# Outputs of a retention layer: the cross product joined with half of the inner one, both query decays moved to 64 partitions, and one turned operand given its own memory

## The chip, the cores and the metric

The kernel runs on 1 core of one Trainium2 chip. The metric is the device time of one execution in microseconds (us). Engines are named as the profile names them: PE (TensorE, matmul), PEld (its weight loads), DVE (VectorE), ACT (ScalarE), POOL (GpSimd), SP (SyncE, which issues most DMAs).

## The reference, cut to what matters

x is 4 sequences of 1024 tokens by 1024 channels. A layer norm gives xn. From xn come a ternary-weight product with a SiLU (the gate g) and a retention layer s; the result is x + s * g. The retention layer works over 16 heads of 64 dimensions in chunks of 128 tokens, with a state S of 64 x 64 per head that passes from chunk to chunk:

```python
mask  = where(t >= s, exp(-s_h * (t - s)), 0)          # per head, 128 x 128, lower triangle
lam_t = exp(-s_h * t); lam_rev = exp(-s_h * (T - t)); lam_T = exp(-s_h * T)
scores = einsum('bhtd,bhsd,hts->bhts', qi, ki, mask)
intra  = einsum('bhts,bhsd->bhtd', scores, vi)
cross  = einsum('bhtd,ht,bhde->bhte', qi, lam_t, S)
o      = scale * (intra + cross)
S      = lam_T * S + einsum('bhtd,ht,bhte->bhde', ki, lam_rev, vi)
```

The output o is normalised (RMS, twice, folded into one scale per token), projected by ternary weights and multiplied by the gate.

## The kernel before, in words

The 4096 tokens are worked in 16 blocks `i` of 256 tokens, each of 2 chunks `c` of 128 tokens; `g = 2 i + c` numbers the chunks. A sequence is 8 chunks (4 blocks). Chunks 0, 8, 16 and 24 are first in their sequence and have no state to take over; so 28 of the 32 chunks have a cross product. Blocks 0 to 2 are worked in one order, from block 3 on in another ("by tokens"), and in blocks 4 to 14 the projection is done by 7 products instead of 8 ("by products").

Each engine has its program written out by hand, in order, with semaphores between them. In one block from 4 on, PE does: the q projections of the block (L854), the k and v products (L839, L813) mixed with the projection of the block before (L1012), then for c = 0: `scores` (L892, q times k, transposed: source tokens are partitions, query tokens are columns), a v and an ffn product (L813, L787), `turn_k` (L904), `outputs` (L938 and L942), `update_state` (L919), ffn products; then for c = 1: `scores`, an ffn product, `output_scale` (L964: sums of squares of the first chunk's outputs, through `total_of`), ffn products with `spread_gamma` (L973) among them, `outputs`, and the projection of the first chunk. In a block whose first chunk is first in its sequence (4, 8, 12) `output_scale` stands half a product later, and in blocks 3 and 15 a whole product later.

`outputs` makes, for each pair of heads r and each head e of the pair, 64 rows of `att_ps` (64 dimensions by 128 tokens) from two f32 products. The cross product (L938) has `state` as weights, 128 partitions by 64 columns, with zeros in the half of the other head, and `q_decay` as moving operand. The inner product (L942) has `v_tok` (128 tokens by 64 columns) as weights and `scores_m` as moving operand; both move 128 columns. An f32 product stands as two records in the trace.

DVE masks the scores (`mask_scores`, L1523, four instructions a chunk, one for each half of the heads and each e), weights the outputs (`weight_o`, L1581), adds the new part to the state (`add_state`, L1567), splits operands into high and low halves (L1362, L1597), combines rows (L1378, L1608), and finishes k and v (`add_k` L1407, `add_v` L1399). PE's last k product, "p4", waits for the second `add_k` of the block; the last v product "p4" for the second `add_v`; `output_scale` on PE waits for the sums that POOL makes (`sum_squares`, L2506 to L2515).

POOL runs in this order in such a block: `add_out` (L2532), `output_scale` of the block before (L2521, L2525), `norm_scale` of the next block (L2385 to L2404), `decay_q(i, 0)` in two halves (L2481), more `add_out`, `decay_state(i, 0)` (L2493), `bias_z` (L2466, L2468), `decay_q(i, 1)` in two halves, `sum_squares(i, 0)`, `output_scale(i, 0)`, `decay_state(i, 1)`, `sum_squares(i, 1)`. In block 1 POOL also subtracts ffn and v weights (L2416, L2428), which keeps it busy from 144 us on; `decay_q(1, 0)`, `decay_state(1, 0)` and `decay_q(1, 1)` stand in that row ahead of `output_scale(1, 0)`.

`b_turned`, an operand of the k and v products, is written by ACT (`weigh_b`, L2009) and lies in the same memory as `scores_m`.

Of the kernel before, what the change touches and what calls it, by code (L numbers as in the profile page):

```python
# [36 lines left out]
def program(nc, x, qkv_w, proj_w, decay, ffn_w, ffn_b, norm_cols, x_turned, out):  # L37
# [17 lines left out]
    with ExitStack() as ctx:  # L55
# [34 lines left out]
        QL_OFF = V_OFF + CHUNKS * C  # L90
        ST_OFF = QL_OFF + 2 * C
        SM_OFF = ST_OFF + 2 * PR * P
        ARENA = SM_OFF + H * T
# [4 lines left out]
        with nc.sbuf_tensor("arena", [P, ARENA], F32) as arena:  # L98
            pass
        sb("arena_low", [P, SM_OFF])  # L100

        o_row = sb("o_row", [P, CPH, T])
        o_split = sb("o_parts", [P, 3, 2, CPH, T], F16)
# [26 lines left out]
        v_tok = arena[:, V_OFF:QL_OFF].rearrange("p (c n) -> p c n", c=CHUNKS)  # L130
        q_decay = arena[:, QL_OFF:QL_OFF + C].rearrange("p (r t) -> p r t", r=PR)
        k_decay = arena[:, QL_OFF + C:QL_OFF + 2 * C]

        ow_first = k_decay.rearrange("p (r t) -> p r t", r=PR)
        state = arena[:, ST_OFF:SM_OFF].rearrange("p (k r e) -> p k r e", k=2, r=PR)
        scores_m = arena[:, SM_OFF:ARENA].rearrange("p (h e r t) -> p h e r t", h=HALF, e=2, r=CPH)

        b_turned = arena[:, SM_OFF:ARENA].rearrange("p (c j t) -> p c j t", c=CHUNKS, j=NCB)
# [7 lines left out]
        lam_T = sb("lam_T", [P, PR])  # L146
# [13 lines left out]
        diag = sb("diag", [P, CHUNKS, T])  # L160

# [36 lines left out]
        s_state0 = sem("state_zeroed")  # L198
# [138 lines left out]

        def passes_on(g):

            return g - g // NCHUNK  # L340
# [5 lines left out]
        def of_half(i, c, h):  # L346
            return chunk(i, c) * HALF + h + 1

# [347 lines left out]
        def tensor_program(pe):  # L696
# [514 lines left out]
        def vector_program(dve):  # L1211
# [297 lines left out]
            def mask_scores(i, c):  # L1509
# [5 lines left out]
                if c == 0 and i > 0 and by_products(i - 1):  # L1515

                    dve.wait_ge(s_ops, of_o_product(i - 1, "p3"))
                for half in range(HALF):
                    dve.wait_ge(s_sc, HALF * g + half + 1)
# [30 lines left out]
            def add_state(i, c):  # L1550
# [3 lines left out]
                if n == 0:  # L1554
                    dve.wait_ge(s_state0, 1)
# [3 lines left out]
                else:  # L1559
                    dve.wait_ge(s_sd, 2 * (passes_on(g) - (g // NCHUNK + 1)) + 2)  # L1560
# [1234 lines left out]
```

## Time and profile before

| | |
|---|---|
| runs of the kernel | 1314.46 us median of 3 (1314.1 to 1314.81) |
| profiled execution, first to last instruction | 1314.2 us |
| granted TensorE clock over the span | 1.000 |
| PE busy | 1289.1 us (98%) |
| PEld busy | 824.8 us (63%) |
| DVE busy | 1008.4 us (77%) |
| ACT busy | 617.4 us (47%) |
| POOL busy | 600.4 us (46%) |
| share of PE in the chain that ended last | 94% |

Busy time of PE counts every moment in which a matmul is in the array; matmuls overlap, so the duration of one in the rows (its time through the array) is longer than its distance from the next. The chain of work gives the distances. In the timeline, a row is a run of like instructions on one engine: its start, its length, the count, and in brackets the idle time before it with what ended it.

### The profile page before, as it was taken

The page shows a single profiled execution, that of the slowest core. Times are in us where ns is not written, and L with a number is a line of the kernel's source. Part 1 is how long each engine was busy: PE and PEld are TensorE (multiplying, and loading weights), DVE is VectorE, ACT ScalarE, POOL GpSimd, SP SyncE. Part 2 cuts the span into 40 slices and gives each one's busy share as a digit, 9 for nine tenths or more (in the row PEclk, how much of TensorE's full clock was granted, in tenths as well). Part 3 has the DMA queues.
Part 4 walks back from the last instruction along what each step waited for, and adds up shares of the span by engine and source line. Part 5 has one row for each costly group of instructions (what it writes and reads, how often), then busy time and mean ns, then how long its engine had stood idle before and what let it go on. Part 6 is the DMA issues. An engine that isn't in the chain of part 4 may idle for free.

```text
span 1314.2 us, 25908 instructions
## 1 busy us (share of the span) xinstructions
PE 1289.1 (98%) x10263; PEld 824.8 (63%) x10263; DVE 1008.4 (77%) x1567; ACT 617.4 (47%) x1216; POOL 600.4 (46%) x537
## 2 busy tenths in 40 slices
PE   4999999999999999999999999999999999999998
PEld 2577767675665757566574656657566575756655
DVE  7888367687676887878788787877878788787755
ACT  5884144344434635446354544644436363544621
POOL 1442785955354435354432535435333443535352
PEclk9999999999999999999999999999999999999999
DMA  9631101203012030210303011030300304021020
GB/s 361 248 97 66 57 34 37 101 33 106 1 38 100 17 121 18 76 46 18 121 17 120 18 57 65 17 121 18 94 28 19 119 17 121 17 58 49 1 65 32
DMA packets 33433, 90.32 MB, mean 69 GB/s; under 512 B 10529, under 2 KB 10785, under 8 KB 33314
## 3 DMA queue, kind: packets, MB, share of 16 engines
q1 hardware_dynamic: 33024, 88.65, 20.0%
q8 instruction: 82, 1.34, 0.4%
q14 instruction: 37, 0.30, 0.1%
q10 hardware_dynamic: 290, 0.02, 0.0%
HBM read 71.85 MB, written 16.81 MB: 67 GB/s over the span
## 4 chain that ended last, share of the span: by engine, by line
PE 94%; DVE 2%; ACT 2%; DMA 1%; issue 1%; SPq 0%; POOL 0%; DVEq 0%; ACTq 0%; POOLq 0%
PE ring L854 20%; PE ring L787 13%; PE ring L813 13%; PE ring L839 12%; PE ring L1012 10%; PE ring L988 5%; PE att_ps L892 4%; PE att_ps L942 4%; PE att_ps L938 4%; PE ring L904 2%; PE att_ps L919 2%; PE ring L867 1%; PE ring L754 1%; DMA raw<-in_ffn_w 1%; ACT junk L1951 1%
## 5 line engine op out<-in xcount | busy, mean ns | idle before, releaser
L854 PE MATMUL ring<-b_lo,qkv_q 128*128 128x256 f16 x1216 | 268.2, 272 | 0.0
L854 PE MATMUL ring<-b_hi,qkv_q 128*128 128x256 f16 x1216 | 268.2, 273 | 0.0
L2532 POOL TENSOR_TENSOR xt<-xt,gate_even 128x512 f32<-128x512 f32 x58 | 90.6, 1564 | 172.5 <-DVE gate_even L1626 131.8
L854 PEld LDWEIGHTS ring<-b_hi,qkv_q 128*128 128x128 fp8e4 x1216 | 120.2, 99 | 15.8 <-issue 0.4
L854 PEld LDWEIGHTS ring<-b_lo,qkv_q 128*128 128x128 fp8e4 x1216 | 118.9, 98 | 15.6
L2506 POOL TENSOR_TENSOR sq<-sq,cols 128x1024 f32<-128x1024 f32 x29 | 55.0, 1896 | 126.8 <-DVE b_lo L1423 118.6
L2094 ACT ACTIVATE gate_even<-gate_even 128x512 f32<-128x512 f32 x60 | 37.3, 625 | 136.2 <-DVE gate_even L1454 136.1
L942 PE MATMUL att_ps<-arena 128*64 128x128 f32 x1024 | 95.0, 273 | 0.0
L938 PE MATMUL att_ps<-arena 128*64 128x128 f32 x896 | 88.5, 276 | 0.0
L1523 DVE TENSOR_TENSOR arena<-att_ps,mask 128x512 f32<-128x512 f32 x128 | 79.3, 680 | 11.0 <-PE att_ps L892 11.0
L2385 POOL TENSOR_TENSOR ln<-ln,small 128x3 f32<-128x3 f32 x32 | 37.4, 1168 | 100.2 <-DVE ln L1311 99.3
L2481 POOL TENSOR_TENSOR arena<-arena,lam_q 128x512 f32<-128x512 f32 x56 | 77.2, 1398 | 9.7 <-ACT arena L2110 7.0
L1454 DVE SCALAR_TENSOR_TENSOR gate_even<-ring,ln,gate_even 128x512 f32<-128x512 f32 x70 | 52.4, 748 | 29.0 <-PE ring L787 29.0
L2466 POOL TENSOR_TENSOR gate_even<-gate_even,bias 128x512 f32<-128x512 f32 x14 | 19.8, 1415 | 114.0 <-ACT gate_even L2070 113.9
L2110 ACT ACTIVATE arena<-ring,wscale 128x512 f32<-128x512 f32 x64 | 43.4, 679 | 58.0 <-PE ring L854 58.0
L892 PEld LDWEIGHTS att_ps<-arena 64*128 64x128 f32 x1024 | 59.7, 188 | 13.8 <-issue 13.8
L2493 POOL TENSOR_TENSOR arena<-arena,lam_T 64x512 f32<-64x512 f32 x48 | 61.6, 1283 | 13.5 <-DVE arena L1565 10.8
L892 PE MATMUL att_ps<-arena 64*128 64x128 f32 x1024 | 65.8, 278 | 0.5 <-ACT sq L2136 0.5
L1648 DVE SCALAR_TENSOR_TENSOR gate_even<-ring,wscale,gate_even 128x512 f32<-128x512 f32 x36 | 27.0, 749 | 50.7 <-PE ring L1012 36.2
L942 PEld LDWEIGHTS att_ps<-arena 128*64 128x64 f32 x1024 | 63.5, 137 | 0.7 <-issue 0.7
L2521 POOL TENSOR_TENSOR small<-small 128x1 f32<-128x1 f32 x32 | 18.5, 580 | 99.5 <-DVE small L1633 99.5
L787 PE MATMUL ring<-ffn_q,a_lo 128*128 128x512 fp8e4 x168 | 63.6, 379 | 0.0
(298 smaller groups left out, 3523.1 us busy)
## 6 DMA issues: line engine op xcount, KB each, us to landing
xt<-in_x SPq DMA_DIRECT2D x60, 512.0 KB, 3.7
out<-xt SPq DMA_DIRECT2D x31, 512.0 KB, 2.7
raw<-in_qkv_w SPq DMA_DIRECT2D x24, 512.0 KB, 15.8
y<-in_x_turned SPq DMA_DIRECT2D x14, 512.0 KB, 5.9
y_odd<-in_x_turned SPq DMA_DIRECT2D x14, 512.0 KB, 6.7
raw<-in_ffn_w SPq DMA_DIRECT2D x8, 512.0 KB, 9.8
norm_rows<-norm_out SPq DMA_DIRECT2D x14, 256.0 KB, 6.0
raw<-in_proj_w SPq DMA_DIRECT2D x6, 512.0 KB, 4.7
```

Of the source, the lines that this page charges most:

```text
L787: ins = pe.matmul(ring[:, b, :], of[:, j, :], weights_of(weights)[:, j, :], start=(begins and j == 0 and k == 0), stop=(j == CPH - 1 and k ...
L813: ins = pe.matmul(ring[:, b, :], of[:, j, :], v_weights_of(weights)[:, j, :], start=(name in ("p1", "p5") and j == 0 and k == 0), stop=(j ...
L839: ins = pe.matmul(ring[:, b, :], of[:, j, :], k_weights_of(weights)[:, j, :], start=(name in ("p1", "p5") and j == 0 and k == 0), stop=(j ...
L854: ins = pe.matmul(ring[:, b, e * BT:(e + 1) * BT], qkv_q[:, cb, o:o + P], part[:, cb, :], start=(cb == 0 and part is b_hi and (e == 0 or i ...
L892: ins = pe.matmul(att_ps[:, 2 * half + e, j, :], k_t[rows, r, ts], q_t[rows, r, ts], start=True, stop=True)
L938: pe.matmul(att_ps[e * D:(e + 1) * D, half, j, :], state[:, passes_on(g) % 2, r, e * D:(e + 1) * D], q_decay[:, r, :], start=True, stop=Fa ...
L942: ins = pe.matmul(att_ps[e * D:(e + 1) * D, half, j, :], v_tok[:, c, r * P + e * D:r * P + (e + 1) * D], scores_m[:, half, e, j, :], start ...
L988: ins = pe.matmul(ring[:, b, :], part[:, cb, :], proj_q[:, cb, cs], start=(cb == 0 and k == 0), stop=(cb == NCB - 1 and k == 1))
L1012: ins = pe.matmul(ring[:, b, :], of[:, j, :], proj_weights_of(weights)[:, j, :], start=(name in ("p1", "p5") and j == 0 and k == 0), stop= ...
L1523: dve.tensor_tensor(scores_m[:, half, e, :, :], att_ps[:, 2 * half + e, :, :], mask[:, e, half * CPH:(half + 1) * CPH, :], ALU.mult).then_ ...
L2481: pool.tensor_tensor(q_decay[:, hs, :], q_t[:, hs, c * T:(c + 1) * T], lam_q[:, hs, :], ALU.mult).then_inc(s_ql, 1)
L2532: pool.tensor_tensor(o, o, gate_of(i)[:, c, cs], ALU.add).then_inc(s_add, 1)
```

## The change

For a chunk that is not first in its sequence, a new buffer `v_state` holds, per head, 64 tokens of v on partitions 0 to 63 and the head's state on partitions 64 to 127. A new buffer `stack` holds per head three pieces of 64 columns: piece 0 has the masked scores of the early 64 query tokens (partitions 0 to 63; the early queries see no later sources) over the decayed q of the early tokens (partitions 64 to 127); piece 1 the masked scores of the late 64 query tokens on all 128 partitions; piece 2 zeros over the decayed q of the late tokens. One product of `v_state` over pieces 0 and 2 (128 columns) gives the cross product of all tokens and the inner product of the early ones; one product of v over piece 1 (64 columns) adds the inner product of the late ones.

The state now lies on partitions 64 to 127 for both heads of a pair, without the zeros. `decay_q` becomes two POOL instructions on 64 partitions by 1024 elements, one per head of the pair, both after the whole outputs of the chunk before; `decay_state` becomes one instruction of 64 partitions by 1024 instead of two of 64 by 512. The first 64 tokens of v are copied into `v_state` by a DMA of 256 KB that ACT issues, one for each such chunk. `b_turned` gets its own memory, and `weigh_b` no longer waits for the outputs of the block before.

```diff
             def outputs(i, c, half):
...
-                if not is_first(g):
-                    pe.wait_ge(s_ql, HALF * takes_over(g) + half + 1)
-                    if half == 0:
-                        pe.wait_ge(s_st, 2 * passes_on(g))
+                if not is_first(g) and half == 0:
+                    pe.wait_ge(s_ql, 2 * takes_over(g) + 2)
+                    pe.wait_ge(s_st, 2 * passes_on(g))
+                    pe.wait_ge(s_vcopy[c], copied(i, c))
...
-                    if not is_first(g):
+                    to = [att_ps[e * D:(e + 1) * D, half, j, :].rearrange("p (s t) -> p s t", s=2) for e in range(2)]
+                    v = [v_tok[:, c, r * P + e * D:r * P + (e + 1) * D] for e in range(2)]
+                    if is_first(g):
                         for e in range(2):
-                            pe.matmul(att_ps[e * D:(e + 1) * D, half, j, :],
-                                      state[:, passes_on(g) % 2, r, e * D:(e + 1) * D], q_decay[:, r, :],
-                                      start=True, stop=False, skip_group_check=True)
+                            ins = pe.matmul(to[e], v[e], stack[:, e, r, 0:2, :], start=True, stop=True)
+                        continue
+
                     for e in range(2):
-                        ins = pe.matmul(att_ps[e * D:(e + 1) * D, half, j, :],
-                                        v_tok[:, c, r * P + e * D:r * P + (e + 1) * D],
-                                        scores_m[:, half, e, j, :], start=is_first(g), stop=True,
-                                        skip_group_check=True)
+                        pe.matmul(to[e], joined(g)[:, r, e, :], stack[:, e, r, 0:3:2, :],
+                                  start=True, stop=False, skip_group_check=True)
+                    for e in range(2):
+                        ins = pe.matmul(to[e][:, 1, :], v[e], stack[:, e, r, 1, :],
+                                        start=False, stop=True, skip_group_check=True)
...
             def mask_scores(i, c):
...
+                early = slice(0, P if is_first(g) else D)
...
-                    for e in range(2):
-                        dve.tensor_tensor(scores_m[:, half, e, :, :], att_ps[:, 2 * half + e, :, :],
-                                          mask[:, e, half * CPH:(half + 1) * CPH, :], ALU.mult).then_inc(s_scm, 1)
+                    for s, rows in enumerate((early, slice(0, P))):
+                        ts = slice(s * D, (s + 1) * D)
+                        dve.tensor_tensor(stack[rows, :, hs, s, :], att_ps[rows, 2 * half:2 * half + 2, :, ts],
+                                          mask[rows, :, hs, ts], ALU.mult).then_inc(s_scm, 1)
...
             def add_state(i, c):
...
                 for e in range(2):
-                    rows, cs = slice(e * D, (e + 1) * D), slice(e * D, (e + 1) * D)
-                    to = state[rows, (n + 1) % 2, :, cs]
+                    rows = slice(e * D, (e + 1) * D)
+                    to = v_state[D:P, (n + 1) % 2, :, e, :]
...
             def weigh_b(i, c):
 
-                act.wait_ge(s_o, HALF * (chunk(i - 1, 1) + 1))
+                if c == 0 and i > 2:
+                    act.wait_ge(s_bslo, of_b_sum(i - 1, "S4"))
+                    if by_products(i - 2):
+                        act.wait_ge(s_ops, of_o_product(i - 2, "p3"))
...
+            def copy_v(i, c):
+
+                g = chunk(i, c)
+                if is_first(g):
+                    return
+                for by in v_at(i, c):
+                    act.wait_ge(*by)
+                if g > 1:
+                    act.wait_ge(s_o, HALF * (g - 1))
+                else:
+                    act.wait_ge(s_wout, w_n["qkv", QKV_TILES - 1])
+                act.dma_start(joined(g)[0:D, :, :, :].rearrange("p r e d -> p (r e d)"),
+                              v_tok[0:D, c, :]).then_inc(s_vcopy[c], DMA)
...
             def attention_by_tokens(i, c):
                 if c == 0:
                     take_v(i, 1)
+                    copy_v(i, 1)
                     base_z(i)
...
-            def decay_q(i, c, half):
+            def decay_q(i, c):
                 g = chunk(i, c)
                 if is_first(g):
                     return
-                n = takes_over(g)
-                hs = slice(half * CPH, (half + 1) * CPH)
-                pool.wait_ge(s_q, CPH * i + 2 * (half + 1))
...
-                if n > 0:
-                    pool.wait_ge(s_o, HALF * (g - 1) + half + 1)
-                pool.tensor_tensor(q_decay[:, hs, :], q_t[:, hs, c * T:(c + 1) * T], lam_q[:, hs, :],
-                                   ALU.mult).then_inc(s_ql, 1)
+                pool.wait_ge(s_q, CPH * (i + 1))
...
+                pool.wait_ge(s_o, HALF * g)
...
+                for e in range(2):
+                    rows = slice(e * D, (e + 1) * D)
+                    q, by = (of.rearrange("p r (s t) -> p r s t", s=2)
+                             for of in (q_t[rows, :, c * T:(c + 1) * T], lam_q[rows, :, :]))
+                    pool.tensor_tensor(stack[D:P, e, :, 0:3:2, :], q, by, ALU.mult).then_inc(s_ql, 1)
+                    pool.wait_ge(s_ql, 2 * takes_over(g) + e + 1)
...
             def decay_state(i, c):
...
-                for e in range(2):
-                    rows, cs = slice(e * D, (e + 1) * D), slice(e * D, (e + 1) * D)
-                    pool.tensor_tensor(state[rows, (n + 1) % 2, :, cs], state[rows, n % 2, :, cs],
-                                       lam_T[rows, :].unsqueeze(2).to_broadcast([D, PR, D]), ALU.mult).then_inc(s_sd, 1)
-
-                    pool.wait_ge(s_sd, 2 * (n - g // NCHUNK - 1) + e + 1)
+                to, of = (v_state[D:P, k % 2, :, :, :].rearrange("p r e d -> p (r e) d") for k in (n + 1, n))
+                pool.tensor_tensor(to, of, lam_T[D:P, :].unsqueeze(2).to_broadcast([D, H, D]),
+                                   ALU.mult).then_inc(s_sd, 1)
+                pool.wait_ge(s_sd, decays(g))
```

In blocks from 3 on, `copy_v(i, 0)` stands on ACT's queue behind the high parts of the next block's b and ahead of `take_v(i, 1)`. No call on POOL's queue moves: `decay_q(i, c, 0)` and `decay_q(i, c, 1)` become `decay_q(i, c)` where they stood.

## Rows read from the trace of the kernel before

**Rows 1.** The page: the chain that ended last, shares by engine.
```profile
PE 94%; DVE 2%; ACT 2%; DMA 1%; issue 1%; SPq 0%; POOL 0%; DVEq 0%; ACTq 0%; POOLq 0%
```

**Rows 2.** The chain of work in block 6: start us, us, what.
```profile
573.06 0.22 PE att_ps L942 x4
573.28 0.93 PE att_ps L919 x32
574.21 3.56 PE ring L787 x16
```

**Rows 3.** POOL's instructions by line and shape: busy us, mean ns of one.
```profile
L2493 POOL TENSOR_TENSOR arena<-arena,lam_T 64x512 f32<-64x512 f32 x48 | 61.6, 1283 | 13.5 <-DVE arena L1565 10.8
L2506 POOL TENSOR_TENSOR sq<-sq,cols 128x1024 f32<-128x1024 f32 x29 | 55.0, 1896 | 126.8 <-DVE b_lo L1423 118.6 <-ACT sq L2136 8.2
L2510 POOL TENSOR_TENSOR sq<-sq 128x512 f32<-128x512 f32 x29 | 36.8, 1271 | 2.3
L2510 POOL TENSOR_TENSOR sq<-sq 128x256 f32<-128x256 f32 x29 | 21.1, 729 | 2.3
```

**Rows 4.** Timeline of POOL, block 6, chunk 0 to chunk 1.
```profile
573.20 2.51 POOL L2481 TENSOR_TENSOR arena<-arena,lam_q 128x512 f32<-128x512 f32 x2
575.66 1.90 POOL L2506 TENSOR_TENSOR sq<-sq,cols 128x1024 f32<-128x1024 f32 x1
579.86 0.46 POOL L2515 TENSOR_TENSOR sq_sum<-sq 128x128 f32<-128x128 f32 x1
583.66 2.16 POOL L2493 TENSOR_TENSOR arena<-arena,lam_T 64x512 f32<-64x512 f32 x2
```

**Rows 5.** Timeline: PE's output_scale in blocks 6 and 4, POOL's last sum in 4.
```profile
581.45 0.38 PE L964 MATMUL att_ps<-small,sq_sum 128*128 128x1 f32 x2
423.71 0.45 POOL L2515 TENSOR_TENSOR sq_sum<-sq 128x128 f32<-128x128 f32 x1
424.43 0.28 PE L964 MATMUL att_ps<-small,sq_sum 128*128 128x1 f32 x2
```

**Rows 6.** Timeline of POOL, DVE and PE, start of block 6.
```profile
537.94 2.94 POOL L2481 TENSOR_TENSOR arena<-arena,lam_q 128x512 f32<-128x512 f32 x2
537.97 1.78 DVE L1378 TENSOR_TENSOR y_odd<-y,y_odd 128x512 f32<-128x512 f32 x1
539.67 1.75 DVE L1362 TENSOR_TENSOR a_lo<-y,a_hi 128x512 f16<-128x512 f32 x1
542.17 0.68 DVE L1362 TENSOR_TENSOR a_lo<-y,a_hi 128x512 f16<-128x512 f32 x1
546.63 0.74 DVE L1407 SCALAR_TENSOR_TENSOR gate_odd<-ring,wscale,gate_odd 128x512 f32<-128x512 f32 x1
547.97 0.38 PE L839 MATMUL ring<-k_sum_last,b_hi 128*128 128x512 fp8e4 x1
551.63 0.75 DVE L1648 SCALAR_TENSOR_TENSOR gate_even<-ring,wscale,gate_even 128x512 f32<-128x512 f32 x1 [2.87 <-PE ring L1012]
```

**Rows 7.** Timeline of POOL and PE in block 1.
```profile
189.05 0.38 POOL L2525 TENSOR_SCALAR diag<-ident,small 128x128 f32<-128x128 f32 x1
190.03 0.49 PE L973 MATMUL ring<-diag,mean_sq 128*128 128x128 f32 x2
```

**Rows 8.** Timeline of block 7: DVE's split of o, then PE's next product.
```profile
666.73 1.22 DVE L1597 TENSOR_TENSOR o_lo<-arena,o_hi 128x1024 f16<-128x1024 f32 x1
668.21 0.39 PE L1012 MATMUL ring<-proj_q,o_hi 128*128 128x512 fp8e4 x1
```

**Rows 9.** DMA issues of the page: count, KB each, median us to landing.
```profile
out<-xt SPq DMA_DIRECT2D x31, 512.0 KB, 2.7
y_odd<-in_x_turned SPq DMA_DIRECT2D x14, 512.0 KB, 6.7
```

**Rows 10.** Timeline of DVE and PE around outputs of block 6, chunk 0.
```profile
563.68 1.40 DVE L1399 SCALAR_TENSOR_TENSOR arena<-ring,wscale,arena 128x512 f32<-128x512 f32 x2
569.57 0.44 PE L938 MATMUL att_ps<-arena 128*64 128x128 f32 x4
```

More of the change, by code:

```diff
@@ L97, in program @@
             pass
[L98 to L103, printed above, removed]
+        arena = sb("arena", [P, ARENA])
         SQ = 2 * PR * T
@@ L160, in program @@
         diag = sb("diag", [P, CHUNKS, T])
+        with nc.sbuf_tensor("b_turned", [P, CHUNKS, NCB, T], F32) as b_turned:
+            pass
+        o_row = sb("o_row", [P, CPH, T])
+        o_split = sb("o_parts", [P, 3, 2, CPH, T], F16)
         wsum = diag[:, 0, 0:5 * NCB]
@@ L197, in program @@
         s_ident, s_iota, s_cut = sem("ident_made"), sem("iotas_made"), sem("mask_cut")
-        s_state0 = sem("state_zeroed")
+        s_zeros = sem("stack_zeros_set")
+        s_vcopy = [sem(f"v_copied{c}") for c in range(CHUNKS)]
         s_ones, s_peak = sem("constants_set"), sem("peak_taken")
@@ L336, in is_last, with decays @@
             return g % NCHUNK == NCHUNK - 1
+        def decays(g):
+            return sum(not is_first(k) and not is_last(k) for k in range(g + 1))
         def passes_on(g):
@@ L347, in of_half, with copied, joined @@
             return chunk(i, c) * HALF + h + 1
+        def copied(i, c):
+            return DMA * sum(not is_first(chunk(k, c)) for k in range(i + 1))
+        def joined(g):
+            return v_state[:, passes_on(g) % 2, :, :, :]
         def of_ffn(i, c, h):
@@ L1514, in mask_scores @@
                     dve.wait_ge(s_wout, w_n["qkv", QKV_TILES - 1])
-                if c == 0 and i > 0 and by_products(i - 1):
-                    dve.wait_ge(s_ops, of_o_product(i - 1, "p3"))
+                early = slice(0, P if is_first(g) else D)
                 for half in range(HALF):
+                    hs = slice(half * CPH, (half + 1) * CPH)
                     dve.wait_ge(s_sc, HALF * g + half + 1)
@@ L2108, in qk_out @@
                     elif j == 0:
-                        act.wait_ge(s_ql, HALF * takes_over(chunk(i, 0)))
+                        act.wait_ge(s_ql, 2 * takes_over(chunk(i, 0)))
                     act.activation(q_t[:, r:r + 2, :], bank, ACT.Copy, scale=wscale[:, 7:8]).then_inc(s_q, 1)
@@ L2473, in decay_q @@
                     return
[L2474 to L2477 removed]
+                pool.wait_ge(s_q, CPH * (i + 1))
+                if takes_over(g) == 0:
                     pool.wait_ge(s_tables, TABLES)
[L2479 to L2482 removed]
+                pool.wait_ge(s_o, HALF * g)
+                if c == 1:
+                    pool.wait_ge(*((s_zeros, 1) if i == 0 else (s_vwsum, 3) if i == 1 else (s_zbias, HALF * (i - 1))))
+                elif i + 1 == NB:
+                    pool.wait_ge(s_gamma, chunk(i - 1, 1) + 1)
+                elif by_products(i - 1):
+                    pool.wait_ge(s_beta, chunk(i + 1, 1) + 1)
+                else:
+                    pool.wait_ge(*((s_pwsum, 1) if i == BY_PRODUCTS - 1 else (s_add, of_out(i - 1, 1, 1))))
+                for e in range(2):
[4 more added lines that the diff above has]
+                    pool.wait_ge(s_ql, 2 * takes_over(g) + e + 1)
             def decay_state(i, c):
@@ L2559, in attention @@
                             sum_v_weights(name)
-                    decay_q(i, 1, 0)
-                    decay_q(i, 1, 1)
+                    decay_q(i, 1)
                 else:
@@ L2605, in gpsimd_program @@
             pool.wait_ge(s_wout, w_n["qkv", QKV_TILES - 1])
-            pool.memset(state, 0.0).then_inc(s_state0, 1)
+            pool.memset(stack[0:D, :, :, 2, :], 0.0).then_inc(s_zeros, 1)
             for i in range(NB):
@@ L2624, in gpsimd_program @@
                     if by_products(i - 1):
-                        decay_q(i, 0, 0)
-                        decay_q(i, 0, 1)
+                        decay_q(i, 0)
                         add_out(i - 1, 1, 1)
@@ L2639, in gpsimd_program @@
                             sum_proj_weights("T4")
-                        decay_q(i, 0, 0)
-                        decay_q(i, 0, 1)
+                        decay_q(i, 0)
                 attention(i, 0)
```

42 lines of the change are left out of this document (27 added, 15 removed).

## The prediction

> **What bounds the kernel now.** I read the page's chain of work first: 94% of it is PE [rows 1], and PE is busy for 98% of the span. So a microsecond taken from PE's own work is a microsecond of time, as long as nothing that PE waits for comes later than it does now. Next I read the chain in order of time inside one block (block 6, a middle one), to see what one product costs in distance and not in its pipelined length: two heads with 128 moving columns take 0.22 us, and the 16 products of update_state, weights of the same shape (128 by 64) with 64 moving columns, take 0.93 us together, 0.116 us a pair [rows 2]. Then I read POOL's timeline between the two chunks of a block against PE's [rows 4, 5], because the change puts work on POOL, and last the start of a block, where POOL and DVE meet [rows 6]. The averages (POOL 46% busy, DVE 77%) say nothing here: what matters is how long before PE each result is there. For POOL's sums that is 581.45 less 580.32, 1.1 us, in a middle block, and 424.43 less 424.16, under 0.3 us, in a block that opens a sequence [rows 4, 5].
>
> **What the change takes from PE.** Per pair of heads, two products of 128 columns for two heads (0.22 + 0.22) become one of 128 and one of 64 (0.22 + 0.116): 0.104 saved, 0.83 us for the 8 pairs of a chunk. 28 chunks have a cross product: 23.2 us. The first chunks of the four sequences keep one product of 128 columns and save nothing. Bounds: exactly half of 0.22 would give 24.6 us; if weight loads set the pace the saving is smaller (rival D).
>
> **What it adds to POOL.** decay_q was two instructions of 128 x 512, 2.46 us for both (573.20 to 575.66) [rows 4]. Now it is two of 64 x 1024. What sets a POOL instruction's time is the elements per partition and how many full operands it reads: 256 take 0.729 us and 512 take 1.271, so 2.12 ns an element [rows 3], and 1024 take 1.271 + 512 x 0.00212 = 2.36 us. The number of partitions does not help: with one broadcast operand, 64 x 512 twice takes 2.16 [rows 4], 1.08 each, and 128 x 1024 takes 1.90 [rows 3], again by elements per partition. Two of 2.36, with about 0.1 for the waits that the new code puts behind each, make 4.85 us: 2.4 us more for each call. No row has this shape; the lower bound is 1.90 an instruction (the broadcast form), the upper 2.54 (twice 1.271). decay_state becomes one instruction like the 1.90 row instead of 2.16: 0.26 less.
>
> **Where that lands, between the chunks.** decay_q(i, 1) begins when POOL is free, with no idle time ahead of it [rows 4], so its waiting for the whole of outputs(i, 0) costs nothing (those end 0.8 us earlier than now). What is queued behind it is sum_squares(i, 0), and PE's output_scale waits for that. The sums come 2.4 us later; PE arrives 0.83 us earlier; the slack was 1.1. PE waits 2.4 + 0.8 - 1.1 = 2.1 us in blocks 5, 6, 7, 9, 10, 11, 13 and 14: 17 us. In blocks 4, 8 and 12 outputs(i, 0) save nothing and the slack is under 0.3: 2.2 each, 6.5 us. In blocks 3 and 15 output_scale stands a whole ffn product later (3.56 / 2 = 1.8 us [rows 2]): 0.3 each, 0.6 us. Blocks 0 and 2 have room.
>
> **Block 1** has both calls on a POOL that is never idle. PE's spread_gamma there has 190.03 - 189.43 = 0.6 us of slack [rows 7]; POOL comes to it 2 x 2.4 - 0.26 = 4.5 later. So it falls 3.9 us behind, and the 1.7 that the block's outputs save is swallowed too: 5.6 us of waiting.
>
> **At the start of a block.** decay_q(i, 0) runs beside DVE work in which both inputs lie in SBUF, and DVE is held while a POOL instruction runs: two DVE instructions take 1.78 and 1.75 us where the same form takes 0.68 unhindered [rows 6]. Each POOL instruction holds one of them; with POOL's each 1.1 longer, DVE falls 2.2 us behind. The DVE work up to the second add_k (L1407) is without idle time, and PE's last k product waits for that: it ends at 547.37 and PE starts at 547.97 [rows 6]. So PE waits about 2.2 - 0.55 = 1.65 us, in the blocks 5, 6, 7, 9, 10, 11, 13, 14 that have this order: 13.2 us. After it DVE has 2.87 us of idle time [rows 6], so the lateness goes no further. Bounds: nothing if the collision falls elsewhere, 16 us if the upper POOL price holds. Blocks 2, 3 and 15 have the collision in another place; I take 1 us for them together.
>
> **After outputs(i, 1).** PE's next product in blocks 7 and 11 needs DVE's split of o, which is there 668.21 - 667.95 = 0.26 us ahead [rows 8]; with outputs 0.83 shorter PE waits 0.6 in each, and about 0.4 in blocks 2, 3 and 15: 2.3 us.
>
> **At nothing.** The mask stays four DVE instructions of 512 elements. The adding of the state keeps its shape and writes other partitions. The DMA of v: ACT issues it when add_v of the chunk is done, 564.4 us, and outputs begin at 569.57 [rows 10], 5.1 us later; 512 KB out of SBUF land in 2.7 us, the slowest kind in the rows in 6.7 [rows 9], and this is 256 KB. I take it as hidden; uncovered it would cost up to 1.6 us in some 9 chunks. ACT waits at that point for DVE ahead of take_v(i, 1), whose product isn't ready before. The waits taken from weigh_b and from the first mask of a block are already passed in the order of those queues (ACT squares the outputs of the block before ahead of weigh_b), so b_turned's own memory gives nothing.
>
> For such a copy the Trainium skill (DMA: Bandwidth & Descriptors, Anatomy of one DMA) gives a fixed 2.0 us plus bytes over 436 GB/s, an estimate of 2.6 us here; by it the copy is hidden as well, and no row of this trace has an SBUF-to-SBUF copy.
>
> **Sum.** -23.2 + 17 + 6.5 + 0.6 + 5.6 + 13.2 + 1 + 2.3 = +23.0 us against the profiled span of 1314.2; the median of the runs is 0.3 above it. Forecast 1337 us, 1.7% slower: PE's saving is real and is more than spent in waits for POOL and for DVE held up by POOL.
>
> **Rivals.** *A, POOL late but DVE not held longer.* The 13.2 and the 1 fall away: 1323 us. For it: the collision depends on which engine gets in first. Against: all eight blocks show the same two long DVE rows.
>
> *B, POOL not late (the other side).* If a POOL instruction's time goes by all its elements, 64 x 1024 costs what 128 x 512 did, 1.27, and every wait above but the last goes: 1314.2 - 23.2 + 2.3 = 1293 us, 1.6% faster. It decides at the length of the pair of decays: under 2.7 us (2.46 + what is left of the slack, 1.1 - 0.83) PE does not wait in a middle block; the whole change breaks even with the pair at about 3.75 (some 21 pairs on the path share the 23 us). Against it speaks that 64 x 512 is no cheaper per column than 128 x 1024 [rows 3, 4]. At the lower bound of 1.90 each the pair is 0.9 shorter: 11 x 0.9 + 1.8 + 8 x 0.9 off the sum, about +4 us, 1318.
>
> *C, the copy of v is late.* With 6.7 us to landing outputs(i, 0) start 1.6 later in 9 chunks; most of it comes off the wait at output_scale behind it, so some +4 us: 1341.
>
> *D, weight loads pace the 64-column product,* so that columns save little. Then the saving before output_scale was lost anyway, and 16 x 0.83 = 13 us in second chunks is not had: about 1348. Against it speaks update_state, same weights and 64 columns, at half the distance [rows 2].
>
> The Trainium skill's rule for a stream of weight load and matmul (TensorE: Matmul & The Clock Gate, Back-to-back issue gap) speaks for D: it gives about 81 ns a matmul at 128 columns and 131 at 512, so 64 columns fewer save some 8 ns of a record. By that estimate 448 products of two records each would save 7 us in place of 23. The trace does not follow it: a record here takes 55 ns at 128 columns and 29 at 64 [rows 2].
>
> **Chances.** The forecast with both waits (1327 to 1345): 0.52. A, or the lower POOL bound with a little of each (1317 to 1327): 0.22. Within 0.2% of before, 1312 to 1317: 0.05. B and partial gains, below 1312: 0.12. C, D and worse, above 1345: 0.09. The range 1311 to 1345 holds 0.8; the likeliest alone has 1327 to 1345. Differences under 0.2% (2.6 us) can't be told from none for this kernel. Faster 0.12, same 0.05, slower 0.83.
>
> **What would show it.** In the profile after: the joined product and the 64-column one at 0.22 and 0.11 to 0.12 a pair in the chain; the decay_q group at 2.3 to 2.5 us mean, 56 of them; idle time on PE ahead of output_scale, released by POOL's sum, about 2 us in 11 blocks; idle time ahead of the last k product, released by add_k, about 1.7 us in 8; DVE's L1378 and L1362 rows near 2.9 us where they were 1.78 and 1.75. The prediction is wrong if POOL's pair takes under 3.75 us, if PE shows no idle time at output_scale, or if the 64-column products stand 0.2 apart.

## The result, and the profile after

The changed kernel takes 1357.18 us (median of 4 runs, 1355.65 to 1358.16); the kernel before, timed beside it, 1314.63 (4 runs). The ratio is 1.032, with a 95% interval from 1.031 to 1.034. The change makes the kernel 3.2% slower. The forecast had the direction, at 1337 us, but the time is 12 us above the top of its range. The profiled execution's span is 1356.9 us, 42.7 more than before.

The page of the changed kernel: busy time of PE, the chain that ended last, two groups of instructions (busy us, mean ns of one, idle time before them) and the DMA of v.

```profile
PE 1289.5 (95%) x10263; PEld 809.5 (60%) x10263; DVE 1032.9 (76%) x1567; ACT 616.4 (45%) x1216; POOL 661.8 (49%) x513
...
PE 58%; DVE 17%; POOL 16%; issue 4%; ACT 2%; DMA 2%; SPq 0%; DVEq 0%; POOLq 0%; ACTq 0%
...
L2531 POOL TENSOR_TENSOR arena<-arena,lam_q 64x1024 f32<-64x1024 f32 x56 | 139.5, 2491 | 26.1 <-PE att_ps L953 11.8
...
L798 PE MATMUL ring<-ffn_q,a_hi 128*128 128x512 fp8e4 x168 | 69.3, 413 | 0.0
...
arena<-arena ACTq DMA_DIRECT2D x28, 256.0 KB, 3.0
```

PE's share of the chain fell from 94% [rows 1] to 58%: the chain now goes through POOL's q decays and DVE's work. PE's waits, in the view of waits (us in total, times, longest):

```profile
PE att_ps L980 <- POOL sq_sum L2569: 25.3, 13, 2.3
PE ring L746 <- DVE y L1339: 12.4, 2, 11.6
PE ring L850 <- DVE gate_odd L1423: 9.3, 8, 1.2
PE ring L989 <- POOL diag L2579: 2.6, 2, 2.1
...
PE att_ps L957 <- POOL arena L2531: 2.1, 1, 2.1
PE ring L824 <- DVE arena L1415: 1.8, 1, 1.8
PE ring L746 <- DVE small L1649: 1.5, 1, 1.5
PE ring L1028 <- DVE o_lo L1613: 1.1, 2, 0.5
```

All waits of that view sum to 64.3 us, and to 22.1 in the same view of the kernel before: 42.2 more. The 12.4 at the start were there before:

```profile
PE ring L735 <- DVE y L1323: 12.5, 2, 11.7
```

But TensorE also saves time, so waits alone don't close the account. What is missing stands in the chain in order of time, between the chunks of block 6 (start us, us, what), where [rows 4, 5] were taken before:

```profile
587.44 2.34 POOL arena L2531
...
589.86 2.36 POOL arena L2531
...
592.28 1.91 POOL sq L2560
...
596.47 0.46 POOL sq_sum L2569
...
597.07 0.35 PE att_ps L980 x2
597.42 4.30 PE ring L798 x12
601.71 0.22 PE att_ps L989 x2
```

PE waits for the last sum until 597.07. Then twelve products take 4.30 us where the same chain of the kernel before has 2.61, which is 0.22 a product, the pace of the sixteen in [rows 2]:

```profile
581.83 2.61 PE ring L787 x12
```

The windows of that stretch (us, then busy time of PE, PEld, DVE, ACT and POOL, each with the number of instructions that touch the window, then granted clock, DMA share and GB/s):

```profile
597.00:598.00 1.00, 0.94 (x5) 0.57 (x6) 0.16 (x1) 0.00 (x0) 0.31 (x1) 0.76 0.00 0
598.00:599.00 1.00, 1.00 (x4) 0.32 (x3) 0.00 (x0) 0.00 (x0) 0.72 (x3) 0.50 0.00 0
599.00:600.00 1.00, 1.00 (x3) 0.29 (x2) 0.00 (x0) 0.00 (x0) 1.00 (x1) 0.50 0.00 0
600.00:601.00 1.00, 1.00 (x4) 0.43 (x3) 0.32 (x1) 0.00 (x0) 0.82 (x1) 0.53 0.00 0
601.00:602.00 1.00, 1.00 (x8) 0.61 (x7) 0.43 (x1) 0.54 (x1) 0.00 (x0) 1.00 0.00 0
```

And one of the same products in the kernel before:

```profile
583.00:584.00 1.00, 1.00 (x6) 0.47 (x5) 0.38 (x1) 0.00 (x0) 0.82 (x3) 1.00 0.00 0
```

PE is busy in every one of these microseconds from 597 on, but from 598 to 601 only 3 or 4 products touch each in place of 6: they start 0.43 apart in the timeline where the kernel before has 0.22. The granted clock is 0.50 there, the lower of TensorE's two levels (1.2 of 2.4 GHz). Going through the whole trace in windows of 1 us, this happens 11 times, and the clock missing (1 less the granted clock, summed) is 1.7 us each time, 18.8 together; before, 0.3, at the very end. Eight of them stand behind waits at output_scale (blocks 5 to 10, 13, 14), and three in blocks 0 and 1. This makes the busy time of PE misleading: it is 1289.5 us although 23 us of columns went away, because products at the lower clock are longer (L798 has a mean of 413 ns; 379 in the last kernel below, whose clock never falls).

The account of the 42.7 us, then: 42.2 of waits, 18.8 of clock, some 3.5 for starting again (the product after a wait takes 0.17 longer in the chain, as in 1.90 for 8 products of L850 where 1.73 is usual, and there are about 21 new waits; an estimate), less 22.7 for the products (28 chunks by 0.81, below): 41.8.

### The profile page after: what moved, and what is told of

Read it like the earlier page. It is cut to its first block, busy times and chain, and to the rows that moved or that the text cites. A ratio compares the mean times of both kernels' runs of the same rounds, so it can differ in the third digit from the quotient of the medians.

```text
span 1356.9 us, 25934 instructions
## 1 busy us (share of the span) xinstructions
PE 1289.5 (95%) x10263; PEld 809.5 (60%) x10263; DVE 1032.9 (76%) x1567; ACT 616.4 (45%) x1216; POOL 661.8 (49%) x513
## 4 chain that ended last, share of the span: by engine, by line
PE 58%; DVE 17%; POOL 16%; issue 4%; ACT 2%; DMA 2%; SPq 0%; DVEq 0%; POOLq 0%; ACTq 0%
PE ring L865 15%; PE ring L824 11%; PE ring L798 8%; PE ring L1028 6%; POOL arena L2531 5%; PE ring L850 5%; PE ring L1004 4%; DVE a_lo L1378 3%; POOL sq L2564 2%; PE att_ps L903 2%; POOL sq L2560 2%; PE att_ps L957 2%; DVE y L1394 2%; POOL gate_even L2507 1%; POOL gate_even L2509 1%
## 5 line engine op out<-in xcount | busy, mean ns | idle before, releaser
L2531 POOL TENSOR_TENSOR arena<-arena,lam_q 64x1024 f32<-64x1024 f32 x56 | 139.5, 2491 | 26.1 <-PE att_ps L953 11.8
L1539 DVE TENSOR_TENSOR arena<-att_ps,mask 128x512 f32<-128x512 f32 (+1 forms) x128 | 79.1, 675 | 10.6 <-PE att_ps L903 10.6
L957 PE MATMUL att_ps<-arena 128*64 128x128 f32 x896 | 80.8, 283 | 2.1 <-POOL arena L2531 2.1
L798 PE MATMUL ring<-ffn_q,a_lo 128*128 128x512 fp8e4 x168 | 69.6, 414 | 0.0
L798 PE MATMUL ring<-ffn_q,a_hi 128*128 128x512 fp8e4 x168 | 69.3, 413 | 0.0
L903 PEld LDWEIGHTS att_ps<-arena 64*128 64x128 f32 x1024 | 59.7, 188 | 13.7 <-issue 13.7
L960 PE MATMUL att_ps<-arena 128*64 128x64 f32 x896 | 65.1, 224 | 0.0
L2564 POOL TENSOR_TENSOR sq<-sq 128x512 f32<-128x512 f32 (+1 forms) x58 | 57.8, 997 | 4.5
L2088 ACT ACTIVATE gate_odd<-ring,wscale 128x512 f32<-128x512 f32 x26 | 17.9, 688 | 90.9 <-PE ring L850 90.9
## 6 DMA issues: line engine op xcount, KB each, us to landing
raw<-in_qkv_w SPq DMA_DIRECT2D x24, 512.0 KB, 15.8
```

Source lines behind the costliest of these rows:

```text
L798: ins = pe.matmul(ring[:, b, :], of[:, j, :], weights_of(weights)[:, j, :], start=(begins and j == 0 and k == 0), stop=(j == CPH - 1 and k ...
L903: ins = pe.matmul(att_ps[:, 2 * half + e, j, :], k_t[rows, r, ts], q_t[rows, r, ts], start=True, stop=True)
L957: pe.matmul(to[e], joined(g)[:, r, e, :], stack[:, e, r, 0:3:2, :], start=True, stop=False, skip_group_check=True)
L1539: dve.tensor_tensor(stack[rows, :, hs, s, :], att_ps[rows, 2 * half:2 * half + 2, :, ts], mask[rows, :, hs, ts], ALU.mult).then_inc(s_scm, 1)
L2531: pool.tensor_tensor(stack[D:P, e, :, 0:3:2, :], q, by, ALU.mult).then_inc(s_ql, 1)
L2564: pool.tensor_tensor(sq[:, 0, 0:m, :], sq[:, 0, 0:m, :], sq[:, 0, m:2 * m, :], ALU.add).then_inc(s_sqw, 1)
```

## The experiments

Each is compared with the kernel before on the same chip, where that took 1314.0 to 1317.3 us, so the ratios are what can be set side by side. Spans are those of the profiled executions.

**1. Keep TensorE busy through the wait.** In `output_scale` of the changed kernel, blocks 4 to 14:

```
+                if by_products(i) and c == 0:
+                    pe.wait_ge(s_alo, of_part(i, "S3"))
+                    for k in range(20):
+                        pe.matmul(att_bank(3)[:, 2 * P:4 * P], part_of("S3")[0][:, 0, :],
+                                  weights_of("T3")[:, 0, 0:2 * P], start=True, stop=True)
                 pe.wait_ge(s_red, sums(chunk(i, c)))
```

> The changed kernel, and in blocks 4 to 14 twenty matmuls of 256 columns whose results nobody reads, issued on TensorE just ahead of its wait for GpSimd's sum of squares of chunk 0. GpSimd and VectorE get no work more. Theory A (the change costs 43 us because GpSimd's longer q decays make TensorE wait 2.1 us in eleven blocks, and TensorE's clock falls to its lower level, 0.50, behind each such wait, worth 1.7 us each): TensorE is busy through the wait, the clock stays at 1.00, and the time falls by 11 x 1.7 = 18 us to some 1339 us, with the sum of squares as late as before. Theory B (the clock has no part in it; the 20 us that the forecast lacks are waits elsewhere): the time stays at 1357, or rises if the twenty matmuls outlast the wait.

Measured: 1344.5 us, ratio 1.021 (1.0195 to 1.0225), 14.0 us less span than the changed kernel (14.7 by the two ratios). PE's timeline in block 6:

```profile
592.39 2.36 PE L982 MATMUL att_ps<-ffn_q,a_hi 128*128 128x256 fp8e4 x20
594.58 0.28 PE L985 MATMUL att_ps<-small,sq_sum 128*128 128x1 f32 x2
594.73 0.38 PE L798 MATMUL ring<-ffn_q,a_hi 128*128 128x512 fp8e4 x1
594.94 0.38 PE L798 MATMUL ring<-ffn_q,a_lo 128*128 128x512 fp8e4 x1
```

And the windows of that stretch, with the clock in the third column from the end:

```profile
592.00:594.00 2.00, 2.00 (x18) 1.50 (x17) 1.08 (x2) 0.00 (x0) 1.78 (x3) 1.00 0.00 0
594.00:596.00 2.00, 2.00 (x15) 1.25 (x14) 0.16 (x1) 0.00 (x0) 1.13 (x3) 1.00 0.00 0
```

The sum comes as late as before, PE does 2.4 us of useless work, and the kernel is faster for it: products stand 0.21 apart again. The eight falls at this place are gone. The one in block 0 is gone too, although PE waits there as before (1.5 and 0.5 us), and block 1 has one stretch of 10.2 us at 0.50 where the changed kernel had two short ones. The missing clock is 5.1 us in place of 18.8, 13.7 less, and the span lost 14.0; the expected 18 had counted a fall at all eleven places. So the clock is shown as a cost of its own, apart from the wait.

**2. Half the q decay.** In `decay_q` of the changed kernel, with the stack zeroed once at the start:

```
-                    pool.tensor_tensor(stack[D:P, e, :, 0:3:2, :], q, by, ALU.mult).then_inc(s_ql, 1)
+                    pool.tensor_tensor(stack[D:P, e, 0:CPH, 0:3:2, :], q[:, 0:CPH], by[:, 0:CPH],
+                                       ALU.mult).then_inc(s_ql, 1)
```

> The changed kernel with both q decays over the first four of the eight head pairs only, so each instruction of GpSimd has 64 x 512 elements instead of 64 x 1024; the q decay of the other four pairs is left out (that part of the stack stays zero). TensorE's products are the same. Theory A (all of the loss is GpSimd's time): the pair of decays falls from 4.9 to 2.5 us, the wait ahead of the output scale and the 0.50 clock behind it go, and the 28 x 0.83 us that TensorE saves are seen whole: 1293 us, 1.6% under the kernel before. Theory B (the joined products or the copy of v cost more than their rows show, or TensorE's saving is eaten by the next wait): the time stays above 1310 us.

Measured: 1301.5 us, ratio 0.988 (0.987 to 0.990), clock 1.000. The waits for the sum fall to 0.5 us in all:

```profile
PE att_ps L980 <- POOL sq_sum L2571: 0.5, 3, 0.2
```

This is the case that rival B describes, brought about by leaving the decay of four of the eight head pairs out; what the new products save is real once POOL's work is short. The 1293 expected was some 6 us too good beyond the 2.3 by which this chip is slower: PE's waits sum to 27.7 us, 5.6 more than before, in small ones for DVE's and POOL's parts, 1.2 and 1.4 us long at the most.

**3. The kernel before, made late.** On POOL:

```
+                for _ in range(times):
+                    pool.tensor_tensor(q_decay[:, 0:CPH, :], q_t[:, 0:CPH, T:2 * T], lam_q[:, 0:CPH, :],
+                                       ALU.mult).then_inc(s_again, 1)
...
+                    repeat_q(i, 3 if by_products(i) else 0)
                     decay_q(i, 1, 0)
                     decay_q(i, 1, 1)
```

> The kernel before, with the first half of chunk 1's q decay written three times more on GpSimd in blocks 4 to 14 (128 x 512 elements, 1.27 us each, 3.8 us in all), ahead of the real one. Nothing of the change is in it. Theory A (lateness of GpSimd alone makes both the wait and the fall of the clock): waits of about 2.7 us in eight blocks and 3.5 us in blocks 4, 8 and 12, together 32 us, and behind each the clock at 0.50 for over 3 us, 11 x 1.7 = 18 us more: about 1365 us. Theory B (the slow stretch behind the wait belongs to the new products or to the changed layout): the waits alone, about 1347 us, and a clock of 1.00.

Measured: 1364.5 us (1359.5 to 1368.5), ratio 1.036 (1.033 to 1.039). The row of the view of waits:

```profile
PE att_ps L965 <- POOL sq_sum L2528: 34.1, 11, 3.8
```

The waits were as expected (34.1 us). The falls were not: 4 of the 11 in the profiled execution, behind the three waits of 3.8 us and behind one of the eight of 2.7 to 2.9. They cost the same 1.7 us each. The profiled execution is the fastest of the four, with a granted clock of 0.995. The others took 5 to 9 us more, and their granted clocks are on record as 0.990, 0.990 and 0.988: 13.6, 13.6 and 16.4 us of missing clock where the profiled one has 6.8, so about 8, 8 and 10 falls by an estimate from the 1.7. So lateness of POOL alone makes both costs, without any of the new products, and the clock's part of it is not the same in each execution.

**4. The sum ahead of the decay.** On POOL in the changed kernel:

```
-                if c == 1:
+                if c == 1 and not by_products(i):
                     sum_squares(i, 0)
...
+                    if by_products(i):
+                        sum_squares(i, 0)
+                        pool.wait_ge(s_red, sums(g))
                     decay_q(i, 1)
```

> The changed kernel with GpSimd's sum of squares of chunk 0 issued ahead of chunk 1's q decay in blocks 4 to 14, all its work kept. Theory A: the 25 us of waits for the sum and the 18 us of lower clock behind them go; TensorE waits instead about 1 us in each of the eleven blocks for the q decays of chunk 1, which end later: 1357 - 43 + 11 = about 1325 us, and 1314 if this wait is hidden. Theory B (the sum was only the first of several late things, and the decays are wanted as early): a wait of over 2 us at the outputs of chunk 1, the clock falls there instead, and the time stays at 1350 us or more.

Measured: 1343.7 us, ratio 1.021 (1.019 to 1.023). Both theories missed the place. The sum is in time, but POOL's `output_scale`, which makes the diagonal that PE wants next, is now what is queued behind the decay (PE's timeline, block 6):

```profile
596.42 0.49 PE L989 MATMUL att_ps<-diag,mean_sq 128*128 128x128 f32 x2 [1.69 <-POOL diag L2579]
```

Eight waits of 1.69 us and three of 2.30 took the place of eleven of 2.1 to 2.3: 4 us less. The rest of the gain is the clock: no fall behind any wait of 1.69, two behind those of 2.30, and missing clock of 5.1 us instead of 18.8. The span is 15.8 us shorter, for a reordering that took only 4 us off the waits. That it was their length that kept the clock up is not shown by this run; run 5 tries shorter waits in another kernel.

**5. Fewer repeats.** As 3, with `repeat_q(i, 2 if by_products(i) else 0)`.

> The kernel before with two repeats of the first half of chunk 1's q decay on GpSimd in blocks 4 to 14 where e3_late had three, 2.54 us in all. The sum of squares is 1.27 us less late than in e3_late, whose waits were 2.7 to 2.9 us in eight blocks and 3.8 in three. Theory A (the clock falls behind some waits of over 2 us and behind none of 1.7 or less): waits of 1.4 to 1.6 us in eight blocks and 2.5 us in blocks 4, 8 and 12, some 20 us, and a fall behind at most the three long ones, 1.7 us each: 1337 to 1342 us on a chip where the kernel before takes 1317. Theory B (any stop of TensorE at this place brings the clock down): 11 falls, 19 us more, 1356 us.

Measured: 1339.1 us, ratio 1.019 (1.017 to 1.020). Waits of 1.37 to 1.56 us with no fall, three of 2.43 with two falls. PE's timeline in blocks 4 and 5:

```profile
427.87 0.56 PE L965 MATMUL att_ps<-small,sq_sum 128*128 128x1 f32 x2 [2.43 <-POOL sq_sum L2528]
509.00 0.35 PE L965 MATMUL att_ps<-small,sq_sum 128*128 128x1 f32 x2 [1.55 <-POOL sq_sum L2528]
```

The windows behind these two waits:

```profile
428.00:429.00 1.00, 1.00 (x4) 0.55 (x5) 0.16 (x1) 0.00 (x0) 0.29 (x1) 0.50 0.00 0
510.00:512.00 2.00, 2.00 (x12) 1.08 (x10) 0.75 (x1) 0.08 (x1) 1.74 (x4) 1.00 0.00 0
```

These are theory A's figures, and they speak against theory B: a stop at this place doesn't always bring the clock down.

**6. The start of the block alone.** The edit of run 2, in chunk 0 only:

```
+                    pool.tensor_tensor(stack[D:P, e, 0:(PR if c else CPH), 0:3:2, :], q[:, 0:(PR if c else CPH)],
+                                       by[:, 0:(PR if c else CPH)],
+                                       ALU.mult).then_inc(s_ql, 1)
```

> The changed kernel with the q decay of chunk 0 of each block over four of the eight head pairs only (the other four are left out and stay zero); that of chunk 1 is whole. Theory A (the 9.3 us of waiting at the last k product come from GpSimd holding VectorE through its longer decays at the start of a block): these eight waits of 1.17 us go, and so do some 3 us of the waits in block 1; the waits for the sum of squares and the low clock behind them stay: 1357 - 12 = about 1345 us. Theory B (the last k product waits for something else that the change moved): 1354 to 1357 us.

Measured: 1346.7 us, ratio 1.022 (1.021 to 1.024), 10.0 us less span. The row of L850 is gone from the view of waits. DVE's timeline in block 6 of the changed kernel:

```profile
551.62 2.84 DVE L1378 TENSOR_TENSOR a_lo<-y,a_hi 128x512 f16<-128x512 f32 x1
554.59 2.61 DVE L1394 TENSOR_TENSOR y<-y_odd,y 128x512 f32<-128x512 f32 x1
```

And the same two in this kernel:

```profile
548.88 1.76 DVE L1378 TENSOR_TENSOR a_lo<-y,a_hi 128x512 f16<-128x512 f32 x1
550.78 1.54 DVE L1394 TENSOR_TENSOR y<-y_odd,y 128x512 f32<-128x512 f32 x1
```

The two DVE rows shrink by 1.1 each with POOL's instructions. So the 9.3 us come from POOL holding DVE, as the prediction had it; the waits at the sum (25.4) and eight falls behind them stay. The 9.3 and the 2.1 at block 1's outputs went, but new waits of 0.3 to 1.4 us for v (L824, 2.2 more) and a longer one at block 1's diagonal (1.2 more) took part of that back. The Trainium skill (SBUF — State Buffer, SBUF: two separate sides) says that a VectorE operation with two SBUF inputs and a GpSimd one share a pair of ports as an exclusive lock, held for the whole instruction; these rows agree, with the DVE row growing by what POOL's grew.

**7. b_turned's memory alone.** The kernel before, with b_turned laid out and its waits changed as in the change:

```
+        with nc.sbuf_tensor("b_turned", [P, CHUNKS, NCB, T], F32) as b_turned:
+            pass
+        o_row = sb("o_row", [P, CPH, T])
...
-                    dve.wait_ge(s_ops, of_o_product(i - 1, "p3"))
...
-                act.wait_ge(s_o, HALF * (chunk(i - 1, 1) + 1))
```

> The kernel before with only this part of the change: b_turned lies in memory that it shares with o's row and parts and no longer with the masked scores, and the waits change as in the change. Theory A (that part gives nothing): the ratio is 1.000 within 0.002. Theory B (it lets ScalarE start b earlier and moves work against VectorE): a difference of more than 3 us either way.

Measured: ratio 0.9999 (0.9990 to 1.0008). This part gives and costs nothing.

**8. The joined product without the long decays.** POOL decays q as before, on 128 partitions, into 4 KB of its own, and ACT copies it down:

```
-        stack = arena[:, SM_OFF:ARENA].rearrange("p (e r s t) -> p e r s t", e=2, r=PR, s=3)
+        stack = arena[:, SM_OFF:ARENA].rearrange("p (e s r t) -> p e r s t", e=2, r=PR, s=3)
+        q_ready = sb("q_ready", [P, 2, PR, D])
...
+            def copy_q(i, c):
...
+                act.wait_ge(s_ql, 2 * takes_over(g) + 2)
...
+                act.wait_ge(s_o, HALF * g)
+                for e in range(2):
+                    act.dma_start(stack[D:P, e, :, 0:3:2, :].rearrange("p r s t -> p s r t"),
+                                  q_ready[e * D:(e + 1) * D, :, :, :]).then_inc(s_qcopy[c], DMA)
```

> The changed kernel, all its work kept, with GpSimd decaying q as the kernel before did (two instructions of 128 x 512 into 4 KB of their own) and two DMAs of 256 KB from ScalarE's queue carrying the result into the lower half of the stack; the stack is laid out so that each DMA writes 2 KB runs. TensorE's products are those of the change. Theory A (the change loses only by GpSimd's longer decays, which delay the sum of squares, hold VectorE, and by the clock behind the waits): the pair is 2.5 us again, the waits at the output scale and at the last k product go, the clock is 1.00, and what TensorE saves is seen: about 1295 us, a ratio near 0.985. Theory B (the copies are late, or ScalarE's issues delay its own work): new waits ahead of the outputs, above 1305 us.

Measured: 1315.2 us, ratio 0.9988 (0.9978 to 0.9997). Both theories hold in part. From block 3 on no wait is over 1 us and the clock is 1.00. But ACT now waits for POOL's decay at the start of the block, and in block 2 that decay stands behind three long sums of weights. From the view of waits:

```profile
PE ring L826 <- ACT ring L2044: 8.6, 2, 8.2
PE att_ps L959 <- DMA arena<-arena: 4.0, 1, 4.0
```

And the window around the wait in block 2, with a clock of 0.57 over 12 us:

```profile
248.00:260.00 12.00, 6.82 (x19) 2.51 (x20) 2.02 (x1) 2.11 (x4) 8.86 (x4) 0.57 0.39 117
```

The places in blocks 1 and 2 lost 12.2 us of waits and 8.5 of clock.

**9. The same, chunk 1's decay into POOL's gap.** On POOL, from block 2 on:

```
+                        decay_q(i, 1)
                         bias_z(i)
...
-                    decay_q(i, 1)
+                    if i < 2:
+                        decay_q(i, 1)
```

> The kernel of the run before it, with chunk 1's q decay moved ahead of the bias of z on GpSimd (from block 2 on), into the 7 us in which GpSimd now waits for ScalarE. Theory A (with decays of 2.5 us the sum of squares is already in time): the same time within 2 us. Theory B (the sum is still the last thing to arrive in some blocks, above all 4, 8 and 12): 1 to 4 us less. Theory C (the decay in the gap holds VectorE's two-input work there, and v is late): some us more.

Measured: 1331.9 us, ratio 1.011 (1.010 to 1.013): theory C, 17 us over run 8 (13.4 between the profiled executions, of which these waits are 12.8). From the view of waits (3.5 us in 8 places in run 8):

```profile
PE ring L826 <- DVE arena L1417: 16.3, 12, 2.6
```

POOL's idle time was not free: DVE scales k with two SBUF inputs there, and its two instructions at L1550 took 4.06 us in block 6 where run 8 had 2.99; the part of v behind them is what PE waits for.

**10. The same as 8, with the decays of blocks 1 and 2 ahead of the work that held them.** On POOL:

```
+                        if i < BY_TOKENS:
+                            decay_q(i, 0)
                         add_out(i - 1, 1, 0)
```

> The kernel e5 (q decayed in 128 x 512 and copied by DMA) with the q decay of chunk 0 of blocks 1 and 2 moved on GpSimd ahead of the two additions that stood before it (and in block 2 ahead of three sums of k's weights, 12 us). In e5 TensorE lost 4.0 us in block 1 and 8.2 us in block 2 behind these two decays, and 8.5 us to the lower clock there. Theory A (these two places are all that kept e5 from showing the saving): 1315 - 20 = about 1295 us, a ratio near 0.984, with a clock of 1.00. Theory B (the work moved behind them is late instead): a new wait in block 1 or 2, 1300 us or more.

Measured: 1300.6 us (1299.4 to 1302.2) against 1314.0, ratio 0.990 (0.988 to 0.991): 1.0% faster than the kernel before, and by the two ratios 4.1% faster than the change. From its page, the chain by engine, two groups and the new DMAs:

```profile
PE 84%; POOL 4%; DVE 3%; issue 3%; DMA 2%; ACT 2%; SPq 0%; ACTq 0%; DVEq 0%; POOLq 0%
...
L2544 POOL TENSOR_TENSOR q_ready<-arena,lam_q 128x512 f32<-128x512 f32 x56 | 76.7, 1391 | 5.9 <-ACT arena L2157 5.8
...
L800 PE MATMUL ring<-ffn_q,a_hi 128*128 128x512 fp8e4 x168 | 63.6, 379 | 0.0
...
arena<-q_ready ACTq DMA_DIRECT2D x56, 256.0 KB, 3.8
```

And its chain in order of time, outputs of block 6, chunk 0:

```profile
566.52 0.37 PE att_ps L959 x4
566.89 0.11 PE att_ps L962 x4
567.00 0.22 PE att_ps L959 x4
567.22 0.12 PE att_ps L962 x4
```

The clock never falls, and PE waits 27.7 us in all, 5.6 more than before. Outputs of block 6, chunk 0, take 2.83 us in the chain where the kernel before has 3.64: 0.81 a chunk. The kernel before has there:

```profile
570.23 0.22 PE att_ps L938 x4
570.44 0.22 PE att_ps L942 x4
```

The 1295 expected was 5 us too low; block 1 still has 2.8 us of waits at its outputs and 1.4 at the split of o.

## Why the prediction was wrong, by its own steps

- **PE's saving, 23.2 us.** Right: 0.22 and 0.11 to 0.12 a pair, 0.81 a chunk for 0.83, read from the last kernel, whose clock never falls. Rival D is refuted. The Trainium skill's rule (TensorE: Matmul & The Clock Gate, Back-to-back issue gap), by which 64 columns fewer hardly save, doesn't hold for products of this shape: a record takes 55 ns at 128 columns and 28 or 29 at 64 (0.22 and 0.11 to 0.12 us for four).
- **POOL's price, 2.36 an instruction and 4.85 a pair.** Right: 2.34 and 2.36 in block 6, where nothing is in the way; 2.49 on average.
- **Waits at output_scale, 17 + 6.5 + 0.6 = 24.1.** Right: 25.3 in 13 places, eleven of 2.1 to 2.3 and 0.3 in blocks 3 and 15. That it hangs on the length of POOL's pair (rival B) is shown by runs 2 and 10, whose pairs near 2.5 make them faster than the kernel before.
- **Block 1, 5.6, and room in block 0.** The total is near, the places are not. Block 1 lost 2.1 at its outputs and 2.1 at the diagonal, less the 1.0 at the split of o that it had before: 3.2. Block 0, where the prediction saw room, lost 1.6, of which 1.5 at a turn of y; this wait is gone in run 2 and still there in run 6, so it comes from chunk 1's decay. Together 4.8.
- **Start of a block, 13.2.** The mechanism is right (run 6) and rival A is refuted; the size is off: 8 waits of 1.17, 9.3. The two held DVE rows, 1.78 and 1.75 before [rows 6], are 2.84 and 2.61 (now a split and then a combination): 1.9 more and not 2.2.
- **1 and 2.3 for the remaining places.** 1.8 in block 3 at L824, while 1.6 of such waits elsewhere went away, so 0.2; and 2.9 after the outputs (L1028 1.1, L1004 1.0, L989 0.8).
- **Rival C** is refuted: the copy lands in 3.0 us, no wait of PE names it. The estimate of 2.6 from the Trainium skill (DMA: Bandwidth & Descriptors, Anatomy of one DMA) is 0.4 short; that section gives its figures for DMAs that GpSimd issues, and this copy is ScalarE's.
- **The sum** is the step that failed. It took each wait for its own length and let PE go on at the clock of before: what the clock does behind a stop was put at nothing, without a reason. In the runs the granted clock stands at 0.50 behind eight of the eleven waits at output_scale and behind waits in the first two blocks three times: 18.8 us. Starting again after each wait costs another 0.17, some 3.5 us by the estimate above. The waits came out 4 us less than the 46.2 forecast, the saving 0.5 less: 23.0 - 4.0 + 0.5 + 18.8 + 3.5 = 41.8, and the span grew by 42.7. The 0.09 for times above 1345 was given to rivals C and D, and neither came. None of the signs named for a wrong prediction came up, since none of them was about the clock; and the stretches of [rows 2 to 8] could not show what the clock does behind a stop, as PE never stops there for a microsecond.

What stays open is which waits bring the clock down. The counts are in the last section; the length of the wait alone doesn't tell, and the same kernel has a different number of falls from one execution to the next.

## What to carry to other kernels

When a change makes the bounding engine stop in the middle of a dense stretch, price the stop at its length plus what the trace shows of the clock behind such stops, and look for stops of that length (here from about 2 us, 1.7 us dearer each in most cases but not in all), since shortening a stop or filling it can gain more than is taken off the wait. Work moved onto POOL is priced by elements per partition: packing the decay into half of the partitions took its pair from 2.5 to 4.8 us. A DMA that moves the finished result to other partitions cost nothing where the transfer was covered. And an idle stretch of POOL isn't free while DVE reads two SBUF operands beside it (run 9).

## What the runs showed of the hardware that was not expected

- Behind waits of PE of 2.06 to 2.44 us for POOL's sum (in run 4 for the diagonal) in blocks 4 to 14, the clock fell to 0.50 in 20 of 28 cases (8 of 11 in the changed kernel, 8 of 11 in run 6, 2 of 3 each in runs 4 and 5); behind 1.37 to 1.69 us in none of 16, behind 1.17 us at L850 in none of 24 (the changed kernel, runs 1 and 4). But behind 2.7 to 2.9 us (run 3) it fell in 1 of 8, behind 3.8 in 3 of 3, and behind 2.57 us at L826 (run 9) it did not. At the end of block 0 two waits of 1.5 and 0.5 us close together had a fall behind them in the changed kernel and in run 6, and none in runs 1 and 4. So the length of the wait alone does not decide. A fall is 1.7 us of missing clock, at every place that has one by itself.
- The number of falls varies between executions of one kernel: run 3's four lie 9 us apart, with granted clocks from 0.995 to 0.988, where most kernels here stay within 3 us. A count of falls from one trace is one draw, the 1 of 8 above too.
- A DMA within SBUF of 256 KB on ACT's queue lands in 3.0 us when it writes rows of 4 KB, and in 3.8 us (two at a time) when it writes pieces of 2 KB.
